# Mixing products split in stacked rows, and scans of two chunks behind a zero column with the initial state written by ScalarE into PSUM

## The chip, the cores and the metric

The kernel runs on one core of a Trainium2 chip. The metric is the device time of one launch in microseconds (us); lower is better. A core has five engines with queues of their own: TensorE (PE in the rows, its weight loads PEld), VectorE (DVE), ScalarE (ACT), GpSimd (POOL) and SyncE (SP), which here issues the DMAs. They meet through semaphores.

## The reference

A batch of 16 items (256 tokens of 512 channels, fp32) goes through a layer of self-attention, cross-attention and MLP, and then through an RWKV layer. Only the RWKV layer is touched. What matters of it, for one item (`L` = 256 tokens, 32 heads of 16 channels):

```python
xa = _ln(x)                                   # layer norm
sx = shifted(xa) - xa
t = tanh((xa + sx * maa_x) @ maa_w1).reshape(B, L, 5, 32)
m = einsum('blfd,fdc->blfc', t, maa_w2)       # five mixing products, 32 deep
xw, xk, xv, xr, xg = (xa + sx * (maa_j + m_j) for each j)
w = exp(-exp(time_decay + tanh(xw @ decay_w1) @ decay_w2))
r, k, v, g = xr @ Wr.T, xk @ Wk.T, xv @ Wv.T, silu(xg @ Wg.T)
def step(s, (k, v, w, r)):                    # scan over the 256 tokens
    a = k[..., :, None] * v[..., None, :]     # 16 x 16 per head
    out = einsum('bhs,bhst->bht', r, faaaa * a + s)
    return a + w[..., None] * s, out          # starts from s0
y = group_norm(outs);  x = x + y * g @ Wo.T;  then a gated channel mixing (fWk, fWr, fWv)
```

## The kernel before

Four phases run one after the other: self-attention (names `s_`), cross-attention (`x_`), MLP (`b_`) and RWKV (`c_`). The first three end at 2427 us and are left as they are; all that follows is in `phase_c`.

`phase_c` is a software pipeline over items, written out by hand. Call k of `body` does four parts: "wkv" is the recurrence of item k, "back" is what comes behind it for item k-1 (group norm, Wo, channel mixing, store), "front" prepares item k+1 (mixing products, projections), and "norm" prepares item k+2 (layer norm, shift, and `t`, the input of the mixing products). Calls k = -2, -1, 0 fill the pipeline, a hardware loop does k = 1 to 12 two at a time, and k = 13 to 16 are written out again; 14 and 15 lack "norm" and "front" in turn.

Each call has 16 steps, n = 0 to 15, one for each value channel of a head. A step has two halves i = 0, 1 (chunks 0-1 and 2-3 of the four chunks of 128 channels). Half (n, i) goes so: TensorE copies value channel n of each head to all 16 rows of the head, into the PSUM tile `vb` (L1649); VectorE multiplies by `kT` in place (L1478) and runs the recurrence along the 256 tokens with one scan for each chunk (L1483), which writes the states behind the initial one (`S[..., 1:T + 1]`) and reads the initial state `s0` as its operand. ScalarE puts the initial state in front, once a step (L1359). GpSimd multiplies all four chunks by `rT` (L1205), and TensorE sums over each head's rows, two steps at a time (L1660).

Between the halves, TensorE fills the four PSUM buffers `ps` in turn with everything else. Table `FILLS` (L926) sets which product stands in which step: its first list between the two halves of a step, its second behind the second half. Each fill waits until the use four before it has been emptied. ScalarE and VectorE empty the fills in the same order: what stands in the second list of step n is emptied in step n+1. The names: `g0/g1` silu gate, `mw mk mr mv mg` mixing products, `k r v` projections, `dec1 dec2` decay, `bonus`, `y` centring, `zT`, `o` Wo, `xcT`, `kk rr kv` channel mixing, `xaT` and `t`.

The mixing products (L1586) are fp32 products of `mix2` (32 to 96 rows of weights, zero where they don't belong, and a row of biases) with `tT` (tanh outputs in 96 and 64 rows and a row of ones). TensorE does an fp32 product in two instructions. The `vb` products have `float32r` operands and take one instruction; there the operand is a high part and a low part on different partitions, joined by one product. Group norm (at n = 2) is a chain through four engines: `y` to ScalarE, a sum on VectorE (L1497, L1499), a square root on ScalarE (L1367, with a table load), a reciprocal on VectorE (L1506), then five instructions of GpSimd (L1168 to L1177), and `zT` on TensorE.

SyncE's queue in a call is: load `x5`, load `s0`, load the next item's input, stack the parts of v (three DMAs), store the output. The order is fixed in `body` at L1123.

## Time and profile before

| | |
|---|---|
| median of 3 runs | 4285.62 us (4283.87 to 4286.47) |
| the profiled execution | 4279.43 us, span 4276.5 us |
| phases | attention and MLP to 2427 us; RWKV 2430 to 4276 us |
| busy over the span | PE 87%, DVE 70%, ACT 48%, POOL 41% |
| call to call of the RWKV loop | 104.3 us (L1497: 1564.1 us over 15 calls) |

The span is the stretch from the first to the last instruction of one profiled execution. A row of the timeline gives start, duration, engine, line, what is written and read, and in brackets how long the engine had been idle and what ended that. Consecutive instructions of one kind are merged (x8); an fp32 matmul counts as two. Ends of matmuls are modelled, so a duration of PE overlaps the next start: distances between starts are the safer measure.

### The profile page before, as it was taken

Reading aid. Unit: us, or ns where it says so; the run is one execution under the profiler, and the core shown is the slowest. Engines: PE = TensorE matmul, PEld = TensorE weight load, DVE = VectorE, ACT = ScalarE, POOL = GpSimd, SP = SyncE. Lnnn points to the kernel's source line nnn. Section 1 sums busy time; section 2 is a strip of 40 time slices with the busy share of each in tenths; the row PEclk is TensorE's granted clock in tenths of the full one; section 3 lists DMA queues with packets and bytes.
Section 4 is the critical chain, followed back from the end, with each engine's and each line's share of the span. In section 5 each row is a group of like instructions: output and inputs, shape, how many; then the busy total and the mean of one; then the engine's idle time right before and its main releaser. Section 6 shows DMA issues by size and latency. Waiting matters only on the chain. (4 is left out here: it accounts for less than half of the span.)

```text
span 4276.5 us, 71639 instructions
## 1 busy us (share of the span) xinstructions
PE 3728.2 (87%) x21636; PEld 2870.8 (67%) x21636; DVE 2997.0 (70%) x6732; ACT 2056.6 (48%) x5384; POOL 1740.5 (41%) x1210
## 2 busy tenths in 40 slices
PE   5998898588888886999999778999999999999976
PEld 5777777467777765899999655666666666666643
DVE  5777777477777774655655338878787877888872
ACT  4777777466767674545545422333333333333322
POOL 2444444234344341000000125666666666666652
PEclk9999999699999997999999888999999999999987
DMA  3434434244444434001001110000000000000000
GB/s 110 104 98 108 103 96 104 84 124 115 108 106 110 118 103 125 30 29 44 29 29 44 61 60 18 23 24 23 24 23 24 23 24 23 24 23 23 23 18 15
DMA packets 146611, 256.58 MB, mean 60 GB/s; under 512 B 27184, under 2 KB 32048, under 8 KB 145424
## 3 DMA queue, kind: packets, MB, share of 16 engines
q1 hardware_dynamic: 146448, 254.49, 21.9%
q8 instruction: 92, 1.51, 0.1%
q14 instruction: 71, 0.58, 0.0%
HBM read 107.62 MB, written 33.55 MB: 33 GB/s over the span
## 5 line engine op out<-in xcount | busy, mean ns | idle before, releaser
L1205 POOL TENSOR_TENSOR c_S<-c_S,c_rT 128x1024 f32<-128x1024 f32 x256 | 557.6, 2178 | 468.1 <-DVE c_S L1483 441.9
L1483 DVE TENSOR_TENSOR_SCAN c_S<-c_wT,c_s,c_vb 128x256 f32<-128x256 f32 x1024 | 708.8, 734 | 45.0 <-issue 2.7
L1478 DVE TENSOR_TENSOR c_vb<-c_kT,c_vb 128x512 f32<-128x512 f32 x512 | 352.2, 688 | 296.2 <-PE c_vb L1649 265.9
L348 POOL TENSOR_TENSOR x_prob<-x_prob,x_rsums 128x512 f32<-128x512 f32 x256 | 274.7, 1073 | 480.5 <-DVE x_rsums L510 480.5
L348 POOL TENSOR_TENSOR s_prob<-s_prob,s_rsums 128x512 f32<-128x512 f32 x256 | 274.7, 1073 | 442.0 <-DVE s_rsums L510 442.0
L1649 PE MATMUL c_vb<-c_vhl,c_spread 128*128 128x512 f32 x512 | 301.2, 598 | 73.1 <-DVE c_S L1483 60.1
L404 ACT ACTIVATE x_prob<-x_t,x_tmin 128x256 f32<-128x256 f32 x512 | 256.4, 502 | 220.5 <-DVE x_tmin L503 220.5
L404 ACT ACTIVATE s_prob<-s_t,s_tmin 128x256 f32<-128x256 f32 x512 | 256.4, 502 | 202.9 <-DVE s_tmin L503 202.9
L866 PE MATMUL b_ps<-b_ln_high,b_w_high 128*128 128x256 f32 x1024 | 290.5, 284 | 14.7 <-DVE b_ln_low L808 14.7
L867 PE MATMUL b_ps<-b_ln_low,b_w_high 128*128 128x256 f32 x1024 | 290.5, 284 | 0.0
L868 PE MATMUL b_ps<-b_ln_high,b_w_low 128*128 128x256 f32 x1024 | 290.4, 284 | 0.0
L499 DVE SCALAR_TENSOR_TENSOR s_ps_s<-s_ps_s,s_mask 128x512 f32<-128x512 f32 x256 | 177.7, 694 | 102.0 <-PE s_ps_s L596 74.9
L499 DVE SCALAR_TENSOR_TENSOR x_ps_s<-x_ps_s,x_mask 128x512 f32<-128x512 f32 x256 | 177.7, 694 | 97.0 <-PE x_ps_s L596 77.8
L1163 POOL TENSOR_TENSOR c_xmix<-c_xmix,c_xaT 128x1024 f32<-128x1024 f32 x80 | 173.9, 2174 | 144.6 <-DVE c_xmix L1427 133.2
L764 ACT ACTIVATE b_shared<-b_ps,w_cols 128x256 f32<-128x256 f32 x256 | 123.2, 481 | 207.4 <-PE b_ps L868 205.5
L503 DVE CUSTOM_DVE_ANT_0 x_t<-x_ps_s,x_mneg 128x256 f32<-128x256 f32 x512 | 197.1, 422 | 31.0 <-issue 3.3
L503 DVE CUSTOM_DVE_ANT_0 s_t<-s_ps_s,s_mneg 128x256 f32<-128x256 f32 x512 | 197.1, 422 | 29.3
L606 PE MATMUL x_ps_t<-w_ident,x_prob 128*128 128x128 f32 x1024 | 160.9, 280 | 63.2 <-ACT x_probT L414 52.2
L866 PEld LDWEIGHTS b_ps<-b_ln_high,b_w_high 128*128 128x128 f32 x1024 | 197.2, 193 | 15.7 <-ACT b_ln_high L752 15.1
L866 PE MATMUL b_ps<-b_w_high,b_act_high 128*128 128x512 f32 x512 | 201.7, 394 | 6.2 <-DVE b_act_low L829 6.1
L606 PE MATMUL s_ps_t<-w_ident,s_prob 128*128 128x128 f32 x1024 | 163.5, 284 | 45.2 <-ACT s_probT L414 36.8
L867 PE MATMUL b_ps<-b_w_low,b_act_high 128*128 128x512 f32 x512 | 199.5, 390 | 0.0
(266 smaller groups left out, 10548.7 us busy)
## 6 DMA issues: line engine op xcount, KB each, us to landing
s_stack<-s_parts_qk SPq DMA_DIRECT2D x384, 128.0 KB, 2.4
x_stack<-x_parts_qk SPq DMA_DIRECT2D x384, 128.0 KB, 2.4
s_x_in<-in_x SPq DMA_DIRECT2D x16, 512.0 KB, 3.6
s_xb<-in_x SPq DMA_DIRECT2D x16, 512.0 KB, 4.0
x<-s_x_out SPq DMA_DIRECT2D x16, 512.0 KB, 4.7
x_enc<-in_ctx SPq DMA_DIRECT2D x16, 512.0 KB, 4.4
x_x_in<-x SPq DMA_DIRECT2D x16, 512.0 KB, 3.7
x_xb<-x SPq DMA_DIRECT2D x16, 512.0 KB, 4.2
```

Of the source, the lines that this page charges most:

```text
L348: nc.gpsimd.tensor_tensor(prob[:, h % 4, :, :], prob[:, h % 4, :, :], rsums[:, h, :].unsqueeze(2).to_broadcast([P, TC, T]), ALU.mult).then ...
L404: op = nc.scalar.activation(prob[:, n % 4, tc, :], t[:, n % 2, tc, :], ACT.Exp, bias=tmin[:, n, tc:tc + 1], scale=-1.0, accum_out=psums[:, ...
L499: nc.vector.scalar_tensor_tensor(ps_s[:, n % 2, :, :], ps_s[:, n % 2, :, :], -SCALE, mask[:, :, :], ALU.mult, ALU.mult)
L503: op = nc.vector.tensor_tensor_reduce(out=t[:, n % 2, tc, :], in0=ps_s[:, n % 2, tc, :], in1=mneg[:, tc, :], scale=1.0, scalar=3.0e38, op0 ...
L606: op = nc.tensor.transpose(ps_t[:, h % 2, kc, tc * P:(tc + 1) * P], prob[:, h % 4, tc, kc * P:(kc + 1) * P], w["ident"][:, :])
L866: nc.tensor.matmul(out, sh, mh, start=start, stop=False)
L867: nc.tensor.matmul(out, sh, ml, start=False, stop=False)
L868: return nc.tensor.matmul(out, sl, mh, start=False, stop=stop)
L1205: nc.gpsimd.tensor_tensor(S[:, n % 4, :, 0:T], S[:, n % 4, :, 0:T], rT[:, par, :, :], ALU.mult).then_inc(z_ready, 1)
L1478: nc.vector.tensor_tensor(pair(vb, i), pair(kT[:, par, :, :], i), pair(vb, i), ALU.mult)
L1483: op = nc.vector.tensor_tensor_scan(S[:, n % 4, c, 1:T + 1], wT[:, par, c, :], vb[:, c, :], s0[:, par, c, n:n + 1], ALU.mult, ALU.add)
L1649: nc.tensor.matmul(pair(vb, i), spread[:, place, :], pair(vhl[:, par, slab, :, :], i), start=True, stop=True).then_inc(vb_filled, 1)
```

## The change

Three things change, all in `phase_c`.

1. The mixing products become single `float32r` products. ScalarE writes tanh into `t_low` and a rounded copy into `t_high`; VectorE leaves the difference in `t_low`; SyncE copies high, low and high parts of each of the five groups of 32 rows on top of each other into `tS` (15 DMAs of 32 rows, `stack_t`), and the weights stand in `mix2` as high, high, low, with two rows of biases. The first mixing product of the next call, `mw0`, waits for all 15 (`t_stacked`). `t` and `kv1` change places in `FILLS`.
2. The recurrence runs both chunks of a half in one scan over 512 elements. Column 0 of `wT` is zero, so the running value restarts in each chunk, and the initial state is an element of `vb`: ScalarE copies it into PSUM behind each `vb` product (`start_state`, twice a step), and VectorE's multiply waits for ScalarE (`a0_ready`) and no longer for TensorE.
3. At the start, the mixing weights are loaded three times over into a staging area (15 DMAs of 32 rows) and the biases with two DMAs of 2560 single elements; ScalarE rounds them and VectorE forms the low part before either begins with the first item. Weights wait in groups, and halving fWv moves from the end of call -2 to the end of call -1.

```diff
-             13: (["xaT0", "xaT1"], ["rr0"]), 14: (["rr1"], ["kv0"]), 15: (["kv1"], ["t"])}
+             13: (["xaT0", "xaT1"], ["rr0"]), 14: (["rr1"], ["kv0"]), 15: (["t"], ["kv1"])}
...
-        tT = sb("tT", P, 2, T)
+        MIXROWS = 3 * DM + 2
+        tS = sb("tS", MIXROWS, NMIX, T, dtype=F32R)
...
-        S = sb("S", P, 4, KC, T + 1)
+        S = sb("S", P, 4, KC, T)
...
+        t_low, t_high = b1[:, 0:2, :], b1[:, 2:4, :].bitcast(F32R)
...
-        mix2 = sb("mix2", P, NMIX, C)
+        mix2 = sb("mix2", MIXROWS, NMIX, C, dtype=F32R)
+        mix2_in = S[0:MIXROWS, :, :, :].rearrange("p b c n -> p (b c n)")[:, 0:NMIX * C]
...
 SyncE
+                for place in range(3):
+                    for block, n in ((0, 4), (1, 1)):
+                        for j in range(4 * block, 4 * block + n):
+                            sp.dma_start(staged[DM * place:DM * place + DM, j, :],
+                                         d["maa_w2"][DM * j % P:DM * j % P + DM, block, :]).then_inc(mix2_loaded, 16)
+                at = COL_AT["maa_w"]
+                for row in (3 * DM, 3 * DM + 1):
+                    sp.dma_start(mix2_in[row:row + 1, :].rearrange("o (j n) -> o j n", n=P),
+                                 d["cols"][:, at:at + NMIX * KC].rearrange("p (o j) -> o j p", o=1),
+                                 allow_slow_non_contiguous=True).then_inc(mix2_loaded, 16)
...
+                def stack_t(b):
+
+                    sp.wait_ge(tl_ready, b + 1)
+                    for j in range(NMIX):
+                        rows = slice(DM * (j % 3), DM * (j % 3) + DM)
+                        for place, x in ((0, t_high.bitcast(F32)), (1, t_low), (2, t_high.bitcast(F32))):
+                            sp.dma_start(tS[DM * place:DM * place + DM, j, :].bitcast(F32),
+                                         x[rows, j // 3, :]).then_inc(t_stacked, 16)
...
                         stack_v(k + 1, 1 - par)
+                    if "norm" in parts:
+                        stack_t(k + 2)
                     if "back" in parts:
                         sp.wait_ge(out_ready, k)
...
 GpSimd
-                            pool.wait_ge(a0_ready, step(k, n))
                             pool.wait_ge(scanned, half(k, n, 1))
-                            nc.gpsimd.tensor_tensor(S[:, n % 4, :, 0:T], S[:, n % 4, :, 0:T], rT[:, par, :, :],
+                            nc.gpsimd.tensor_tensor(S[:, n % 4, :, :], S[:, n % 4, :, :], rT[:, par, :, :],
...
 ScalarE
+                act.wait_ge(mix2_loaded, 16 * (3 * NMIX + 2))
+                nc.scalar.copy(mix2[:, :, :].rearrange("p j n -> p (j n)"), mix2_in).then_inc(mix2_high, 1)
...
-                    act.wait_ge(weights_loaded["fWv"], 16)
+
+                def half_of_last():
+                    act.wait_ge(weights_loaded[WEIGHT_GROUP["fWv"]], group_loaded("fWv"))
...
-                        nc.scalar.activation(tT[0:3 * DM, 0, :], unit(name)[0:3 * DM, 0:T], ACT.Tanh)
-                        nc.scalar.activation(tT[0:2 * DM, 1, :], unit(name)[0:2 * DM, T:2 * T], ACT.Tanh).then_inc(done, 1)
+                        for i, rows in ((0, 3 * DM), (1, 2 * DM)):
+                            op = nc.scalar.activation(t_low[0:rows, i, :], channels(name)[0:rows, i, :], ACT.Tanh)
+                        op.then_inc(done, 1)
+                        nc.scalar.drain()
+                        for i, rows in ((0, 3 * DM), (1, 2 * DM)):
+                            op = nc.scalar.copy(t_high[0:rows, i, :], t_low[0:rows, i, :])
+                        op.then_inc(th_high, 1)
...
-                def start_state(k, n, par):
-
-                    if n == 0:
+                def start_state(k, n, i, par):
+
+                    if n == 0 and i == 0:
                         act.wait_ge(s0_loaded, 16 * k + 16)
-                    if not first(k) or n >= 4:
-                        act.wait_ge(summed, k * (RS // 2) + ((n - 4) // 2 + 1))
-                    nc.scalar.copy(S[:, n % 4, :, 0], s0[:, par, :, n]).then_inc(a0_ready, 1)
+                    act.wait_ge(vb_filled, half(k, n, i))
+                    nc.scalar.copy(pair(vb, i)[:, :, 0], s0[:, par, 2 * i:2 * i + 2, n]).then_inc(a0_ready, 1)
 
                 def body(k, parts, par):
                     for n in range(RS):
+                        if "wkv" in parts:
+                            start_state(k, n, 0, par)
                         if n > 0:
                             take(k, FILLS[n - 1][1], parts, par)
...
                         if "wkv" in parts:
-                            start_state(k, n, par)
+                            start_state(k, n, 1, par)
                         take(k, FILLS[n][0], parts, par)
...
                     if isinstance(k, int) and k == -2:
                         late_weights()
+                    if isinstance(k, int) and k == -1:
+                        half_of_last()
...
 VectorE
+                dve.wait_ge(mix2_high, 1)
+                low = mix2[2 * DM:3 * DM + 1, :, :].rearrange("p j n -> p (j n)")
+                nc.vector.tensor_tensor(low, mix2_in[2 * DM:3 * DM + 1, :], low, ALU.subtract).then_inc(mix2_ready, 1)
...
-                        dve.wait_ge(s0_loaded, 16 * k + 16)
                         dve.wait_ge(w_ready, k + 1)
-                    dve.wait_ge(vb_filled, half(k, n, i))
-                    nc.vector.tensor_tensor(pair(vb, i), pair(kT[:, par, :, :], i), pair(vb, i), ALU.mult)
+                    x = pair(vb, i)[:, :, 1:T]
+                    dve.wait_ge(a0_ready, half(k, n, i))
+                    nc.vector.tensor_tensor(x, pair(kT[:, par, :, :], i)[:, :, 0:T - 1], x, ALU.mult)
                     nc.vector.drain()
...
-                    for c in (2 * i, 2 * i + 1):
-                        op = nc.vector.tensor_tensor_scan(S[:, n % 4, c, 1:T + 1], wT[:, par, c, :], vb[:, c, :],
-                                                          s0[:, par, c, n:n + 1], ALU.mult, ALU.add)
-                    op.then_inc(scanned, 1)
+                    nc.vector.tensor_tensor_scan(flat(pair(S[:, n % 4, :, :], i)), flat(pair(wT[:, par, :, :], i)),
+                                                 flat(pair(vb, i)), 0.0, ALU.mult, ALU.add).then_inc(scanned, 1)
...
                         take(k, FILLS[n][0], parts, par)
+                        if n == 15 and "norm" in parts:
+                            dve.wait_ge(th_high, k + 3)
+                            for i, rows in ((0, 3 * DM), (1, 2 * DM)):
+                                op = nc.vector.tensor_tensor(t_low[0:rows, i, :].bitcast(F32R), t_low[0:rows, i, :],
+                                                             t_high[0:rows, i, :], ALU.subtract)
+                            op.then_inc(tl_ready, 1)
...
 TensorE
                         if name == "mw0":
-                            pe.wait_ge(emptied["act"], units.emptied(k + 1, "t"))
-                            pe.wait_ge(mix2_loaded, 16 * NMIX * (KC + 1))
+                            pe.wait_ge(mix2_ready, 1)
+                            pe.wait_ge(t_stacked, 16 * 3 * NMIX * k + 2 * 16 * 3 * NMIX)
                         j = "wkvrg".index(what[1])
-                        rows = 3 * DM + 1 if j < 3 else 2 * DM + 1
                         for a in range(2):
                             c = 2 * i + a
-                            op = nc.tensor.matmul(u[:, a, :], mix2[0:rows, j, c * P:(c + 1) * P], tT[0:rows, j // 3, :],
+                            op = nc.tensor.matmul(u[:, a, :], mix2[:, j, c * P:(c + 1) * P], tS[:, j, :],
                                                   start=True, stop=True)
```

TensorE around the change of calls in the loop, before (L1576 is `t`, the second L1556 row `kv1`, L1549 with Wg `g1`, L1586 `mw0`):

```order
L1660 MATMUL c_acc<-c_S,c_gather 32x512 x4
L1556 MATMUL c_ps<-c_fWv,c_b 128x512 x4
L1647 REGISTER_ALU
L1649 MATMUL c_vb<-c_vhl,c_spread 128x512
L1576 MATMUL c_ps<-c_xmix,c_maa_w 96x256 x4
L1576 MATMUL c_ps<-c_xmix,c_maa_w 64x256 x4
...
L1649 MATMUL c_vb<-c_vhl,c_spread 128x512
...
L1549 MATMUL c_ps<-c_xmix,c_Wg 128x256 x8
L1649 MATMUL c_vb<-c_vhl,c_spread 128x512
L1580 REGISTER_ALU
L1586 MATMUL c_ps<-c_tT,c_mix 128x256 x2
```

The same place in the changed kernel, under its own line numbers (L1617 is `t`, L1597 `kv1`, L1590 `g1`, L1626 `mw0`):

```order
L1700 MATMUL c_acc<-c_S,c_gather 32x512 x4
L1617 MATMUL c_ps<-c_xmix,c_maa_w 96x256 x4
L1617 MATMUL c_ps<-c_xmix,c_maa_w 64x256 x4
L1687 REGISTER_ALU
L1689 MATMUL c_vb<-c_vhl,c_spread 128x512
L1597 MATMUL c_ps<-c_fWv,c_b 128x512 x4
...
L1689 MATMUL c_vb<-c_vhl,c_spread 128x512
...
L1590 MATMUL c_ps<-c_xmix,c_Wg 128x256 x8
L1689 MATMUL c_vb<-c_vhl,c_spread 128x512
L1622 ISA
L1626 MATMUL c_ps<-c_tS,c_mix 128x256 x2
```

Between `t` and `mw0` there were `g1` and two `vb` products; `kv1` and one more `vb` product have moved in behind `t`.

SyncE's queue from the stacking of v to the next load in the loop, in the changed kernel (before, L1137 is not there):

```order
L1121 DMA c_vhl<-c_vhl 64x1024
L1125 DMA c_vhl<-c_vlow 64x1024
L1127 ISA
L1128 DMA c_vhl<-c_vlow 64x1024
L1133 REGISTER_ALU
L1137 DMA c_tS<-c_b 32x256 x15
L1158 DMA out<-c_x 128x2x512
```

The 15 DMAs stand ahead of the store of the output and of the next call's loads.

ScalarE in steps 1 and 2 of the loop, changed kernel (L1388 is `start_state`, L1352 and L1353 empty `y`, L1398 is the square root of group norm):

```order
L1388 COPY c_vb<-c_s 128x2
L1306 REGISTER_ALU
L1352 COPY c_b<-c_ps 128x512
L1353 ACTIVATE c_b<-c_ps 128x512
L1306 REGISTER_ALU
L1352 COPY c_b<-c_ps 128x512
L1353 ACTIVATE c_b<-c_ps 128x512
L1398 ACT_TABLE_LOAD
L1398 ACTIVATE c_grstd<-c_gvar 128x64
L1387 REGISTER_ALU
L1388 COPY c_vb<-c_s 128x2
```

The initial state of half (2, 0) now stands ahead of the emptying of `y`, and that of half (2, 1) behind the square root.

## Rows read from the trace of the kernel before

**Rows 1.** Busy time by stretch: PE, PEld, DVE, ACT, POOL; granted clock, DMA share, GB/s.

```profile
3000.00:3500.00 500.00, 460.16 (x1994) 303.23 (x1994) 399.89 (x631) 158.43 (x365) 305.58 (x175) 0.98 0.08 25
```

**Rows 2.** Timeline of PE, ACT and DVE over one change of calls in the loop.

```profile
3362.03 3.70 PE L1556 MATMUL c_ps<-c_fWv,c_b 128*128 128x512 f32 x8
...
3365.80 3.76 PE L1576 MATMUL c_ps<-c_xmix,c_maa_w 128*96 128x256 f32 x16
...
3369.49 0.50 PE L1649 MATMUL c_vb<-c_vhl,c_spread 128*128 128x512 f32 x1
...
3369.60 0.38 ACT L1297 ACTIVATE c_tT<-c_ps 96x256 f32<-96x256 f32 x1 [11.67 <-PE c_ps L1576]
...
3373.51 1.89 PE L1586 MATMUL c_ps<-c_tT,c_mix 97*128 97x256 f32 x8
...
3375.05 0.59 PE L1649 MATMUL c_vb<-c_vhl,c_spread 128*128 128x512 f32 x1
...
3376.36 0.69 DVE L1478 TENSOR_TENSOR c_vb<-c_kT,c_vb 128x512 f32<-128x512 f32 x1
```

**Rows 3.** The MLP phase's timeline: float32r products of 256 columns.

```profile
1687.27 0.28 PE L867 MATMUL b_ps<-b_ln_low,b_w_high 128*128 128x256 f32 x1
1687.39 0.28 PE L868 MATMUL b_ps<-b_ln_high,b_w_low 128*128 128x256 f32 x1
```

**Rows 4.** Timeline: what PE and DVE wait for between steps 1 and 4.

```profile
3380.27 2.05 PE L1608 MATMUL c_ps<-c_centred,c_b 128*128 128x128 f32 x16 [1.48 <-DVE c_xmix L1427]
...
3387.41 0.70 DVE L1478 TENSOR_TENSOR c_vb<-c_kT,c_vb 128x512 f32<-128x512 f32 x1
3387.53 0.26 ACT L1367 ACTIVATE c_grstd<-c_gvar 128x64 f32<-128x64 f32 x1 [2.62 <-DVE c_gvar L1499]
...
3395.63 1.06 PE L1535 MATMUL c_ps<-w_ident,c_b 128*128 128x128 f32 x8 [0.48 <-POOL c_b L1177]
```

**Rows 5.** Timeline from half (5, 1) to `xcT`: its ends, and half (7, 1).

```profile
3300.24 0.69 DVE L1478 TENSOR_TENSOR c_vb<-c_kT,c_vb 128x512 f32<-128x512 f32 x1 [2.70 <-PE c_vb L1649]
...
3313.80 0.58 PE L1649 MATMUL c_vb<-c_vhl,c_spread 128*128 128x512 f32 x1
...
3314.42 0.70 DVE L1478 TENSOR_TENSOR c_vb<-c_kT,c_vb 128x512 f32<-128x512 f32 x1 [0.35 <-PE c_vb L1649]
...
3320.22 1.25 PE L1535 MATMUL c_ps<-w_ident,c_b 128*128 128x128 f32 x8 [1.58 <-DVE c_xmix L1427]
```

**Rows 6.** Timeline: the two scans of one half.

```profile
3301.01 1.38 DVE L1483 TENSOR_TENSOR_SCAN c_S<-c_wT,c_s,c_vb 128x256 f32<-128x256 f32 x2
```

**Rows 7.** ScalarE's copy of initial states: min/median/max duration in ns.

```profile
L1359 ACT COPY c_S<-c_s x256: 180/187/207, 2532.5 to 4188.9; 128x4 f32<-128x4 f32 x128
```

**Rows 8.** Timeline of SyncE's queue: twelve stacking DMAs of the attention in a row.

```profile
600.62 7.67 SPq L277 DMA_DIRECT2D s_stack<-s_parts_qk  x12
```

**Rows 9.** Loads of mixing weights: min/median/max ns of an issue; us to landing.

```profile
L1098 SPq DMA_DIRECT2D c_mix<-in_maa_w x5: 427/587/587, 2432.5 to 2444.9; - x5
...
DMA to landing us min/median/max: 2.0/2.1/3.2
```

**Rows 10.** Stretches around a wait of TensorE (columns as in rows 1).

```profile
3343.00:3345.70 2.70, 0.00 (x0) 0.00 (x0) 2.55 (x6) 1.95 (x4) 1.42 (x3) 1.00 0.00 0
3345.70:3349.00 3.30, 3.21 (x13) 1.13 (x14) 3.15 (x6) 0.68 (x2) 1.13 (x1) 0.54 0.02 5
```

**Rows 11.** Timeline of the start of the RWKV phase.

```profile
2438.24 1.29 DVE L1409 BATCH_NORM_STATS2 c_ln_stats<-c_xmix 128x6 f32<-128x512 f32 x2 [2.12 <-issue]
...
2452.20 5.23 PE L1576 MATMUL c_ps<-c_xmix,c_maa_w 128*96 128x256 f32 x16 [7.26 <-POOL c_xmix L1220]
...
2458.21 3.69 PE L1586 MATMUL c_ps<-c_tT,c_mix 97*128 97x256 f32 x16 [0.78 <-ACT c_tT L1298]
...
2471.77 1.91 ACT L1258 ACTIVATE c_fWv<-c_fWv 128x2048 f32<-128x2048 f32 x1 [7.38 <-DMA c_fWv<-in_fWv]
2473.77 1.36 PEld L1586 LDWEIGHTS c_ps<-c_tT,c_mix 65*128 65x128 f32 x4 [7.94 <-ACTq L1350]
```

**Rows 12.** A stretch of that start in which mixing weights are loaded (columns as in rows 1).

```profile
2438.60:2441.70 3.10, 0.34 (x2) 0.04 (x1) 1.42 (x6) 0.74 (x2) 0.89 (x2) 0.50 0.22 25
```

More of the change, by code:

```diff
@@ L1319, in move @@
                     elif what == "v":
[L1320 removed]
+                        nc.scalar.copy(pair(vhl[:, other, 0, :, :], i)[:, :, 1:T], channels(name)[:, :, 0:T - 1]).then_inc(vh_ready, 1)
                     elif what == "y":
@@ L1684 @@
              "fWr": (KC, C), "fWv": (KC, C)}
+WEIGHT_GROUP = {n: i for i, names in enumerate((("maa_w1",), ("decay_w1", "decay_w2", "Wk", "Wr", "Wv"),
+                                                ("Wg", "Wo", "fWk", "fWr", "fWv"))) for n in names}
 def build_program(nc, d, out):
```

53 lines of the change are left out of this document (24 added, 29 removed).

## The prediction

> **What bounds the kernel now.** I first read the page (its busy shares stand in the table above), then the busy time by stretch, then the timeline of one call, since the change touches only the RWKV phase. In its loop TensorE is busy 460 of 500 us, VectorE 400, GpSimd 306, ScalarE 158 [rows 1]. That looks like a kernel bound by TensorE, and a change that takes instructions off TensorE looks like pure gain. The timeline says more. The reader should look at who waits in which steps of a call (104.3 us). TensorE waits for VectorE at `y` in step 1 [rows 4], for GpSimd's end of group norm at `zT` in step 4 [rows 4], and for VectorE again at `xcT` in step 8 [rows 5]. Between these places VectorE runs almost without a gap: from half (1, 0), which starts at 3376.36 [rows 2], to half (2, 1) at 3387.41 [rows 4], and from half (5, 1) at 3300.24 to `xcT` at 3320.22, with one wait of 0.35 us at half (7, 1) [rows 5]. So a call is a relay: VectorE and group norm set the pace from the change of calls to `zT`, TensorE from `zT` to half (5, 1), VectorE from there to `xcT`, mostly TensorE after that. The change of calls itself runs without a wait: `t`, then `vb`, `g1`, `vb`, and `mw0` [rows 2].
>
> **What is removed from TensorE, and where it stands.** A call has five mixing products of four matmuls, each in two instructions. Eight of these instructions (`mw0`, `mw1`) take from 3373.51 to 3375.05, 1.54 us [rows 2]; over the x8 row's own 1.89 us at most. After the change four float32r products remain, 0.12 us apart [rows 3], 0.48 us. That is 1.1 us (up to 1.4) for each of five products, 5.5 to 7 us a call. On the path is little of it. `mw` counts, 1.1 us, because half (1, 0) stands behind it. `mk`, `mr` and `mg` lie where TensorE waits for VectorE or for `zT` afterwards [rows 4, 5], and `mv` stands at the head of the VectorE stretch, where its time ends in the 0.35 us wait of half (7, 1).
>
> **What is added at the change of calls.** I count from the end of `t`, the moment at which ScalarE could read it. Before, TensorE spent 3369.49 to 3373.51 on `vb`, `g1`, `vb`, 4.0 us [rows 2]; `kv1` and another `vb` now come in behind `t`, 3362.03 to 3365.80, 3.8 us [rows 2]. That is 7.8 us of cover for the new chain, which goes so:
> - the `vb` product of half (15, 1) and its initial state on ScalarE: 0.6 us from a `vb` to VectorE's start [rows 5], and one copy, 0.19 us [rows 7]: 0.8.
> - VectorE multiplies and scans half (15, 1), 0.7 and 1.3 us [rows 5, 6]; ScalarE's two tanh (0.38 each [rows 2]) and two copies of the same size lie beside it: 2.0.
> - VectorE's two subtractions, of 256 elements; a multiply of 512 takes 0.69 [rows 5], so half of that and a little: 0.4 each, 0.8. SyncE wakes in about 0.1 (my estimate). 3.7 so far.
> - 15 DMAs, issued by one queue. An issue of 32 rows takes 0.43 to 0.59 us [rows 9], and twelve stacking DMAs of the attention, SBUF to SBUF over 32 rows as these are, take 7.67 us, 0.64 each [rows 8]. I take 0.55, between the two: the attention's carry four times the bytes. Fourteen intervals are 7.7 us; the ends are 6.0 and 9.0.
> - the last one lands 2.1 us after its issue [rows 9].
> The sum is 3.7 + 7.7 + 2.1 = 13.5 us against 7.8 of cover: `mw0` waits about 5.7 us (ends 4.0 and 7.0). Behind `mw0` in TensorE's queue stand `mw1`, half (1, 0), the row sums that `y` needs, and all of step 1; VectorE has finished half (0, 1) and `g1` by then and waits too.
>
> TensorE's clock adds to it. After a wait of 2.7 us the granted clock is 0.54 over the next 3.3 us [rows 10], so the half level, 1.2 of 2.4 GHz, for most of them. `mw` and a `vb` then take some 0.4 us more.
>
> So half (1, 0) starts on TensorE at +5.7 - 1.1 + 0.4 = +5.0. On VectorE it was 1.3 us behind TensorE [rows 2] because VectorE was late; it will be 0.9 behind, with ScalarE's hand-over in it: +4.6.
>
> The Trainium skill gives the price of an issue otherwise: "DMA: Bandwidth & Descriptors", Anatomy of one DMA, has about 50 ns of sequencer dispatch, small descriptor generation and a fixed cost of about 2 us, for DMAs issued by GpSimd. The 2 us agree with the trace (2.1), the 50 ns do not (427 to 587 ns on SyncE). By the page's figure the 15 issues would take under 1 us and the chain would be covered; that is rival B below, whose price comes from rows.
>
> **The scans and the initial state.** Two scans of a half take 1.38 us [rows 6]; one over 512 elements saves one instruction's fixed part. Bounds: nothing, and 0.3 us. I take 0.1, since the second scan of the pair starts with the first not yet ended. VectorE had 32 of them a call, 3.2 us, but on the path are the four between half (1, 0) and (2, 1), -0.4, and six up to `xcT`, -0.6. The new hand-over, `vb` to ScalarE to VectorE, is 0.2 to 0.4 us wherever VectorE waits for TensorE: half (5, 1) is on the path, +0.3; the wait of 0.35 at (7, 1) goes, -0.3. Half (11, 1) leads to the late half (13, 0): +0.3 - 0.2. In step 2 ScalarE's state for half (2, 1) stands behind the square root, which ended at 3387.79, while VectorE began that half at 3387.41 [rows 4]; with a copy and a hand-over, +0.7. In steps 3 and 4 the emptying of `dec2` and `zT` moves behind a state each: +0.3. GpSimd loses a wait that did not bind. Sum of this paragraph: +0.1 us.
>
> **Per call:** 4.6 + 0.1 = 4.7 us; 14 calls of the loop and behind it (k = 1 to 14) have `mw0`: +66 us. At k = 0 there is no `kv1` and no half (15, 1): the chain from `t` is 0.7 + 0.7 + 0.8 + 0.1 + 7.7 + 2.1 = 12.1 against 4.0 of cover, 8.1, less 1.1 and with 0.4 as above: +7.
>
> **The start.** VectorE's first statistics began at 2438.24, `t` at 2452.20, `mw0` at 2458.21, and the fifth to eighth of the mixing products waited until 2473.77, because ScalarE stood behind the load of fWv [rows 11]. That wait goes. New: 15 loads of 32 rows at 0.48 to 0.59 us from 2432.5 on end at about 2440.5. Two DMAs of 2560 single elements follow. In 3.1 us before, five DMAs with 512 single elements and 64 KB kept the DMA engines busy 22% [rows 12], 10.9 engine-us; ten times that over 16 engines is 6.8 us, more if fewer engines share it: landed at about 2450. ScalarE's rounding of 2560 columns (2048 took 1.91 [rows 11]): 2.4; VectorE's subtraction of 2560: 2.8. So statistics at 2455, 17 us late, `t` at 2469, `mw0` 18 us behind it instead of 6 (5.3 for `t`, then 12.1) at 2487, and what restarted at 2473.77 comes 8 us behind that: +21 us. Ends: +8 if the elements land with the rest, +45 if they go through few engines.
>
> **Sum:** 66 + 7 + 21 = +94 on the profiled execution's 4279.4 us, 4373; the median of the runs lies 6 us higher, at 4285.6: **4380 us**, slower by 2.2%. The last two calls gain or lose under 5.
>
> **Rivals.**
> A. *TensorE's time counts.* If the busy share tells the truth, a call shortens by the 5.5 to 7 us taken off TensorE and the queue hides its DMAs: 14 x -6 = -84, +15 at the start, 4217 us. For it: 92% busy. Against it: the three waits above, and that the DMAs must all land before the first product.
> B. *The DMAs are covered.* Issues come at 0.1 us, as if no engine's queue held them up; the chain is 3.7 + 1.4 + 2.1 = 7.2 under 7.8 of cover. Then `mw` finds VectorE busy as before, a call changes by about +0.1, and the start is +13: 4300 us.
> C. *The queue is as slow as in the attention and the clock stays low.* 0.64 us an issue, `mw0` waits 7.0, and group norm's square root and row sums run late at 1.2 GHz (1.2 us more): 7.0 - 1.1 + 0.4 - 0.4 + 0.1 + 1.2 = +7.2 a call, 101, with 10 at k = 0 and 35 at the start: 4432 us. It decides from 0.6 us an issue on.
> D. *The start is dearer.* The two element DMAs run through few engines, 45 us: 4404 with the rest as forecast.
>
> **Chances.** Forecast 0.55, A 0.08, B 0.08, C 0.17, D 0.12. The forecast's own range is 4345 to 4415 (issues 0.43 to 0.64, start +10 to +30). The range for 8 in 10 reaches down towards B and up to C: 4310 to 4440. Under 0.2% (9 us) cannot be told from no change; faster by more than that: A, and a little of B, 0.09; within: 0.04; slower: 0.87.
>
> **What would show it.** Right: an idle time of TensorE ahead of `mw0` in each call, 4 to 7 us, ended by a DMA of `tS`; SyncE's 15 issues in a row over 7 to 9 us; a call of 109 us for 104.3; TensorE's busy share down to about 83% in the loop; mixing products 0.12 us apart; a scan of 1.2 to 1.35 us. At the start, `t` near 2469 and the first mixing product near 2487. Wrong: `mw0` without a wait, or a wait there and the time given back between `zT` and `xcT`, which I say is set by VectorE and GpSimd.

## The result and the profile after

The changed kernel takes 4469.4 us (median of 4 runs, 4464.4 to 4478.5) where the kernel before takes 4284.7 in the same job: 1.0439 times as long, 95% interval 1.0418 to 1.0460. Slower was right; the size was not. I had forecast 4380 and a range up to 4440: +94 us, and it is +185.

The profiled execution has a span of 4467.5 us against 4276.5. Its RWKV phase begins 6.8 us later than before, by the earlier phases alone (first load at 2436.99, was 2430.16), so the phase itself lost 184.2. The busy times by stretch of the changed kernel (columns as in [rows 1]):

```profile
3000.00:3500.00 500.00, 427.18 (x1733) 276.39 (x1732) 355.39 (x446) 156.77 (x411) 290.94 (x158) 0.90 0.09 25
```

TensorE went from 460 to 427 us busy in 500, with 1733 instructions for 1994; its granted clock went from 0.98 to 0.90 of full speed. Every engine is busy for less of the time: none of them became the bound, they all wait more.

The change of calls, to be laid beside [rows 2]: TensorE's, VectorE's, GpSimd's and SyncE's rows of the timeline (start, duration, engine, line, what it writes from what; in brackets the idle time before it and who ended it).

```profile
3374.37 3.84 PE L1617 MATMUL c_ps<-c_xmix,c_maa_w 128*96 128x256 f32 x16
...
3378.48 3.59 PE L1597 MATMUL c_ps<-c_fWv,c_b 128*128 128x512 f32 x8
...
3382.14 3.62 PE L1590 MATMUL c_ps<-c_xmix,c_Wg 128*128 128x256 f32 x16
3385.41 0.58 PE L1689 MATMUL c_vb<-c_vhl,c_spread 128*128 128x512 f32 x1
3394.49 1.22 PE L1626 MATMUL c_ps<-c_tS,c_mix 98*128 98x256 f32 x4 [8.51 <-DMA c_tS<-c_b]
```

```profile
3379.64 1.22 DVE L1519 TENSOR_TENSOR_SCAN c_S<-c_wT,c_vb 128x512 f32<-128x512 f32 x1
3380.78 2.90 DVE L1546 TENSOR_TENSOR c_b<-c_b 96x256 fp32r<-96x256 f32 x2
...
3380.94 2.46 POOL L1226 TENSOR_TENSOR c_S<-c_S,c_rT 128x1024 f32<-128x1024 f32 x1 [6.50 <-DVE c_S L1519]
...
3383.70 9.45 SPq L1137 DMA_DIRECT2D c_tS<-c_b  x15
```

The reader should see the chain of the forecast, link by link: `t`, the half (15, 1) on VectorE, the two subtractions, 15 DMA issues in a row, and TensorE with nothing to do for 8.51 us. Two links are longer than I had them. The subtractions take 2.90 us, not 0.8, and they stand beside a multiply on GpSimd. The issues take 9.45, 0.63 each, not 0.55.

The start of the phase (beside [rows 11]), ScalarE, VectorE, TensorE and the DMA queue:

```profile
2446.32 3.29 SPq L1111 DMA_DIRECT2D c_S<-in_cols  x2
2449.64 17.02 SPq L1100 DMA_DIRECT2D c_decay_w<-in_decay_w  x2
...
2474.71 2.32 ACT L1265 CAST c_mix<-c_S 98x2560 fp32r<-98x2560 f32 x1 [30.07 <-DMA c_S<-in_cols]
...
2477.06 2.82 DVE L1439 TENSOR_TENSOR c_mix<-c_S,c_mix 33x2560 fp32r<-33x2560 f32 x1 [33.97 <-ACT c_mix L1265]
2481.98 1.29 DVE L1445 BATCH_NORM_STATS2 c_ln_stats<-c_xmix 128x6 f32<-128x512 f32 x2 [2.10 <-issue]
...
2514.32 2.05 PE L1626 MATMUL c_ps<-c_tS,c_mix 98*128 98x256 f32 x8 [13.18 <-DMA c_tS<-c_b]
```

and the DMA engines in stretches of it (the last two figures are the DMA engines' busy share and GB/s):

```profile
2450.00:2455.00 5.00, 0.00 (x0) 0.00 (x0) 0.00 (x0) 0.00 (x0) 0.00 (x0) 0.50 1.24 1
2455.00:2460.00 5.00, 0.00 (x0) 0.00 (x0) 0.00 (x0) 0.00 (x0) 0.00 (x0) 0.50 1.24 1
2460.00:2465.00 5.00, 0.00 (x0) 0.00 (x0) 0.00 (x0) 0.00 (x0) 0.00 (x0) 0.50 1.33 0
```

The second of the two DMAs of 2560 single elements is issued at 2447.4, and ScalarE, which waits for both, starts at 2474.71, 27 us later. In between the DMA engines move 1 GB/s or less in the stretches shown, with a mean busy share above 1 over the 16 of them (the times of packets overlap, so the share alone does not tell how many engines work). The next load, of decay_w, stays 17 us at the head of the queue, and the norm statistics, which need none of this, stand on VectorE behind the subtraction that waits for it.

To find where a call lost its time I took the starts of TensorE's groups in eleven calls of the loop and the median of each gap (worked out from the timelines; us; the last column is the whole call). `kv1` moved into the first gap and out of the last, 3.8 us.

```
                t-mw0  -y   -dec1  -k0   -zT   -o0   -r0  -bonus -xcT  -v0  ..  -t    call
before           7.7   6.8   3.3   5.3   6.8   5.9   5.7   14.2   4.1  2.4      8.5  105.5
the change      20.1   5.6   3.8   4.0   8.4   7.6   4.5   12.9   5.7  2.6      4.8  115.6
mixing alone    19.9   5.6   3.3   4.0   8.0   5.9   4.5   12.9   6.1  4.2      4.8  114.7
scans alone      7.7   6.6   3.2   5.3   7.6   6.2   5.7   14.2   3.9  2.4      8.5  106.6
all repaired    11.5   6.6   3.8   4.3   8.0   6.0   4.5   12.9   5.7  3.8      4.8  108.3
scans, state
 by VectorE      7.7   6.6   3.2   5.3   6.8   5.9   5.7   14.2   3.8  2.4      8.5  104.5
```

A call gets 8.6 us longer in the first gap (12.4 less the 3.8 of `kv1`). Four other gaps, which hold the five mixing products, get 1.1 to 1.3 us shorter (`mw` and `mk` share the one before `y`). Against that the gaps before `zT`, `o0` and `xcT` get 1.6 to 1.7 us longer each. Before `zT` and `xcT` these are waits for GpSimd and VectorE; before `o0` it is TensorE's clock, as the rows at `zT` will show below.

### The profile page after: what moved, and what is told of

Same layout as the page of the kernel before. It is cut to its first block and busy times, and to the rows that moved or that the text cites. A ratio compares the mean times of both kernels' runs of the same rounds, so it can differ in the third digit from the quotient of the medians.

```text
span 4467.5 us, 71098 instructions
## 1 busy us (share of the span) xinstructions
PE 3720.9 (83%) x21316; PEld 2848.0 (64%) x21316; DVE 2964.6 (66%) x6253; ACT 2101.5 (47%) x5673; POOL 1787.6 (40%) x1212
## 5 line engine op out<-in xcount | busy, mean ns | idle before, releaser
L1226 POOL TENSOR_TENSOR c_S<-c_S,c_rT 128x1024 f32<-128x1024 f32 x256 | 605.1, 2364 | 456.5 <-DVE c_S L1519 456.5
L1388 ACT COPY c_vb<-c_s 128x2 f32<-128x2 f32 x512 | 83.7, 163 | 1232.5 <-PE c_vb L1689 1232.0
L1519 DVE TENSOR_TENSOR_SCAN c_S<-c_wT,c_vb 128x512 f32<-128x512 f32 x512 | 625.0, 1221 | 50.8 <-issue 8.3
L1515 DVE TENSOR_TENSOR c_vb<-c_kT,c_vb 128x510 f32<-128x510 f32 x512 | 351.7, 687 | 455.1 <-ACT c_vb L1388 422.5
L1689 PE MATMUL c_vb<-c_vhl,c_spread 128*128 128x512 f32 x512 | 302.1, 599 | 71.8 <-DVE c_S L1519 56.9
```

The lines of the kernel that those rows point to most:

```text
L1226: nc.gpsimd.tensor_tensor(S[:, n % 4, :, :], S[:, n % 4, :, :], rT[:, par, :, :], ALU.mult).then_inc(z_ready, 1)
L1515: nc.vector.tensor_tensor(x, pair(kT[:, par, :, :], i)[:, :, 0:T - 1], x, ALU.mult)
L1519: nc.vector.tensor_tensor_scan(flat(pair(S[:, n % 4, :, :], i)), flat(pair(wT[:, par, :, :], i)), flat(pair(vb, i)), 0.0, ALU.mult, ALU.ad ...
L1689: nc.tensor.matmul(pair(vb, i), spread[:, place, :], pair(vhl[:, par, slab, :, :], i), start=True, stop=True).then_inc(vb_filled, 1)
```

## The experiments

| kernel | median us | times before (95%) |
|---|---|---|
| the change | 4469.4 | 1.0439 (1.0418 to 1.0460) |
| e1 mixing alone | 4452.8 | 1.0399 (1.0382 to 1.0417) |
| e2 scans alone | 4301.6 | 1.0045 (1.0025 to 1.0064) |
| e3 change, own wait for w | 4405.1 | 1.0281 (1.0258 to 1.0303) |
| e4 change, subtractions early | 4441.9 | 1.0362 (1.0341 to 1.0384) |
| e5 scans alone, rT padded | 4291.6 | 1.0023 (1.0010 to 1.0036) |
| e6 change, rows by transpose | 4443.6 | 1.0384 (1.0366 to 1.0403) |
| e7 change, early and three waits | 4347.8 | 1.0152 (1.0133 to 1.0171) |
| e8 mixing alone, repaired | 4313.3 | 1.0082 (1.0063 to 1.0102) |
| e9 change, all repaired | 4316.9 | 1.0094 (1.0079 to 1.0110) |
| e10 scans, padded, state by VectorE | 4253.8 | 0.9943 (0.9929 to 0.9956) |
| e11 e9 with o1 early | 4317.7 | 1.0094 (1.0078 to 1.0109) |
| e12 before with o1 early | 4280.4 | 1.0007 (0.9997 to 1.0017) |
| e13 change, state by VectorE | 4424.4 | 1.0341 (1.0317 to 1.0364) |
| e14 e9, state by VectorE | 4275.9 | 0.9997 (0.9986 to 1.0009) |
| e15 change, filler of 32 | 4546.4 | 1.0620 (1.0596 to 1.0644) |
| e16 change, filler of 16 | 4454.5 | 1.0428 (1.0408 to 1.0448) |
| e17 scans, state by VectorE | 4268.5 | 0.9977 (0.9967 to 0.9988) |

A hundredth in the ratio is 43 us. Differences between kernels of different jobs are taken from the ratios.

**The two halves alone (e1, e2).** e1 is the change with the lines of `start_state`, `recur`, `S` and the zero columns as before; e2 is the kernel before with those lines of the change.

> The change without its scans: the stacked mixing, the grouped weight semaphores and the exchange of t and kv1 are in, the state still goes into column 0 of S and the scans are two of 256 as before. My theory (the loss lies in the wait for the 15 DMAs that stack t, 8.7 us a call, and in the start): the whole loss stays and the small gain of the merged scans goes, about 4480 us, 1.045 of the kernel before, and the wait of TensorE for tS stays near 8.7 us. Rival (the hand-over of the column through ScalarE, which now stands between TensorE and VectorE in each of 32 halves, costs some 3 us a call): 4420 us or less, and the period of a call falls from 116 to 113 us.

> The kernel before with the scans of two chunks, the zero column and the state written by ScalarE into PSUM, and nothing else; mixing as before. My theory: 0.4 to 0.9 us a call are gained where half-steps wait for each other, 4270 to 4280 us, 0.997 to 0.999 of the kernel before. Rival (the hand-over through ScalarE costs): 4310 to 4335 us, with the period of a call 2 to 3 us longer than 105.8 us.

The stacked mixing costs 171 us by its ratio. The scans, of which I had expected a gain, cost 19 (1.0045), and 17 on top of the mixing (1.0439 less 1.0399). The losses add up. Both of my expectations on the scans were wrong; e2 fell between my range and the rival's.

**The wait for the stacked t (e3, e4, e7).**

```diff
 e3: x[rows, j // 3, :]).then_inc(t_stacked if j else w_stacked, 16)
     mw0 waits for w_stacked, mk0 for t_stacked
 e4: the block "if n == 15 ... tl_ready" moved ahead of recur(k, n, 1, par)
 e7: e4, and three semaphores: j = 0, j = 1, j = 2 to 4;
     ScalarE's copy of y0 waits for the third, since it overwrites t
```

> The change with two semaphores for the stacking DMAs: the first mixing product waits for its own three DMAs alone, and the second group's (k) for the other twelve. My theory: 12 issues of 0.63 us leave the wait of mw0 (8.7 us a call becomes about 1.2) and TensorE keeps its clock; at least 15 x 7.5 = 113 us are gained, up to 150 with the clock: 4320 to 4356 us. What is left over before is then the start (about 50 us) and 1 to 2 us a call. Rival (the landing of a DMA or the late subtraction makes the wait, not the queue of issues): the wait stays above 5 us and the time above 4410 us.

> The change with the two subtractions that make t_low put ahead of VectorE's multiply and scan of half (15,1), so that they no longer stand beside GpSimd's multiply of S and rT. Theory (an operation of VectorE that reads both inputs from SBUF waits while GpSimd works on SBUF): both subtractions together fall from 2.9 to under 1.2 us, t is low 2 to 3 us earlier, and 15 calls gain 30 to 45 us: 4425 to 4440 us. Rival (2.4 us is what the 64x256 subtraction to float32r costs in any place): no gain, 4465 us or more.

> The change with the subtractions ahead of the last half's multiply and with three semaphores for the stacked t: the w product waits for its 3 DMAs, the k product for its 3, the rest for the other 9 (ScalarE's copy of y, which overwrites t, too). Theory (queue of 15 issues and nothing else): from t to the first w product 20.1 us become 11.5 to 12.3, the 9 us from there to y (with one semaphore for the other twelve) become 5.6, the period of a call falls from 116 to 107 to 108, the clock goes back to 0.97, 4469 - 15 x 8 to 9 = 4335 to 4350 us. Rival (VectorE's and GpSimd's chains through the same stretch would be the next wait): period 110 or more, above 4375 us.

e3 gave 68 us by the ratios (1.0439 less 1.0281), not 113: the time from `t` to `mw0` fell by 7.5 us as expected, and 3.4 of them came back between `mw0` and `y` (5.6 to 9.0), because `mk0` waits for the same queue (2.2 us in the call shown, 5.6 in every second one):

```profile
3363.03 0.74 PE L1628 MATMUL c_ps<-c_tS,c_mix 98*128 98x256 f32 x4 [1.34 <-DMA c_tS<-c_b]
...
3370.36 1.22 PE L1628 MATMUL c_ps<-c_tS,c_mix 98*128 98x256 f32 x4 [2.15 <-DMA c_tS<-c_b]
```

In e4 the two subtractions take 0.75 us, and GpSimd's multiply comes after them:

```profile
3372.92 0.75 DVE L1540 TENSOR_TENSOR c_b<-c_b 96x256 fp32r<-96x256 f32 x2 [4.00 <-ACT c_b L1327]
...
3375.65 2.35 POOL L1226 TENSOR_TENSOR c_S<-c_S,c_rT 128x1024 f32<-128x1024 f32 x1 [8.52 <-DVE c_S L1519]
```

That gave 33 us, as expected: the same instructions took 2.1 us less for standing elsewhere. e7, both together, gave 123 us. With it `mw0` and `mk0` have no wait for a DMA left from the second call of the loop on; the first gap is 11.45 us, that is the 7.73 of before and the 3.8 of `kv1`. So the 8.6 us of the first gap were the queue of 15 issues and the late subtraction, and nothing else. One part of what I expected did not come: the granted clock went back to 0.93 only (3000 to 3500), not to 0.97.

**The start (e6).**

```diff
-   sp.dma_start(<row>, d["cols"][...].rearrange("p (o j) -> o j p", o=1))   # 2560 elements, twice
+   TensorE: transpose of the 20 columns; ScalarE: copy to SBUF
+   sp.dma_start(<row>, b2[0:NMIX * KC, 0, 0:P])                             # 20 pieces of 512 bytes, twice
```

> The change, with its two rows of offsets made otherwise: TensorE transposes the 20 columns once, ScalarE copies them out, and each row is loaded by one DMA of 20 pieces of 512 bytes in place of 2560 elements. Theory (the start is long because 2 x 2560 elements are slow and hold the DMA queue, and VectorE's norm statistics stand behind the mixing weights' subtraction): the load is in about 25 us earlier, the statistics start near 2456 instead of 2482, and 25 to 40 us are gained: 4430 to 4445 us. Rival (the start is set by the later weights or by the norm): under 10 us gained.

24 us by the ratios, just under the 25 to 40 that I had expected. From the first load to the first group norm sum the trace has 248.9 us for 272.5. The load of decay_w leaves the queue at once:

```profile
2438.99 1.72 SPq L1111 DMA_DIRECT2D c_S<-c_b  x2
2440.76 1.09 SPq L1100 DMA_DIRECT2D c_decay_w<-in_decay_w  x2
```

**The scans' loss (e5, e10, e17, e13).**

```diff
 e5:  rT = sb("rT", P, 2, KC, T + 1), used in [0:T]
 e10: e5, and in recur, after the wait for vb_filled:
+     nc.vector.tensor_copy(pair(vb, i)[:, :, 0], s0[:, par, 2 * i:2 * i + 2, n])
      start_state and its two calls on ScalarE left out
 e17: e10 without the padding of rT.   e13: the change with e10's copy.
```

> The kernel with the scans alone (4301.6 us, 16.6 above before), with one unused column behind each row of 256 in rT, so that GpSimd's multiply of S and rT has again one operand in separate rows. In the traces GpSimd's 128x1024 multiply takes 2.18 us where S has rows of 257 and 2.36 us where all operands lie close; 16 a call make 2.9 us of GpSimd. Theory 1 (the 17 us come from GpSimd): the multiply takes 2.18 us again and the time falls to 4283 to 4290 us. Theory 2 (they come from the hand-over of the column through ScalarE, ahead of other work of its queue): the multiply may fall, the time stays at 4297 to 4303 us.

> The kernel with the scans alone and rT in padded rows (4291.6 us), but the initial state is copied into the zero column of PSUM by VectorE itself, ahead of its multiply, and ScalarE has no part in it. Theory (what is left over the kernel before, 10 us, is the hand-over TensorE to ScalarE to VectorE in 32 halves a call and what waits behind it in ScalarE's queue): 4270 to 4284 us, at most the kernel before. Rival (the hand-over is free, the copy on VectorE costs its own 0.1 us 512 times): 4292 us or more.

> The change with one edit: VectorE copies the initial state into the zero column itself, ScalarE has no part in it. With the scans alone this edit brought 38 us (4291.6 to 4253.8). Theory (the price of the hand-over is per half-step and holds here too): 4425 to 4440 us. Rival (here the waits for the stacked t set the pace and cover the hand-over): 4455 us or more.

> The scans alone with the state copied by VectorE, rT without its padding, so GpSimd's multiply of S and rT takes 2.36 us again. If the padding is worth what it was beside ScalarE's hand-over (10 us), 4260 to 4268 us against 4253.8 with it. Rival (the padding counted only because ScalarE's queue was late): 4250 to 4257 us.

GpSimd's multiply of S and rT, in the kernel with the scans alone, with the padding, and with VectorE's copy but without padding (grouped instructions: line, operands, count, then busy us and mean ns):

```profile
L1207 POOL TENSOR_TENSOR c_S<-c_S,c_rT 128x1024 f32<-128x1024 f32 x256 | 604.0, 2359 | 438.8 <-DVE c_S L1486 438.8
```

```profile
L1207 POOL TENSOR_TENSOR c_S<-c_S,c_rT 128x1024 f32<-128x1024 f32 x256 | 557.4, 2177 | 456.2 <-DVE c_S L1486 456.0
```

```profile
L1207 POOL TENSOR_TENSOR c_S<-c_S,c_rT 128x1024 f32<-128x1024 f32 x256 | 604.2, 2360 | 442.8 <-DVE c_S L1477 442.6
```

One unused column in rT makes the same multiply 8% faster. It is worth 0.34% without ScalarE's hand-over (e17 against e10). Beside the hand-over it is 0.22% (e5 against e2), between my two theories for e5 and with intervals that overlap, so not shown there by itself. The hand-over is the larger part: taking ScalarE out brings 0.80% (e10 against e5), 0.68% without the padding (e17 against e2), and 0.98% inside the change (e13). One way in which it acts shows at `zT`. First the changed kernel, then e13:

```profile
3416.34 1.36 PE L1576 MATMUL c_ps<-w_ident,c_b 128*128 128x128 f32 x8 [1.79 <-POOL c_b L1199]
...
3417.36 0.78 PE L1689 MATMUL c_vb<-c_vhl,c_spread 128*128 128x512 f32 x1
...
3417.93 4.83 PE L1590 MATMUL c_ps<-c_xmix,c_Wk 128*128 128x256 f32 x16
3418.17 0.16 ACT L1388 COPY c_vb<-c_s 128x2 f32<-128x2 f32 x1 [0.74 <-PE c_vb L1689]
3418.27 1.93 ACT L1296 ACTIVATE c_b<-c_ps,w_cols 128x256 f32<-128x256 f32 x4
...
3420.28 2.35 POOL L1207 TENSOR_TENSOR c_b<-c_b,c_g2T 128x1024 f32<-128x1024 f32 x1 [1.75 <-ACT c_b L1296]
```

```profile
3386.51 1.06 PE L1567 MATMUL c_ps<-w_ident,c_b 128*128 128x128 f32 x8 [1.78 <-POOL c_b L1199]
3387.17 1.93 ACT L1296 ACTIVATE c_b<-c_ps,w_cols 128x256 f32<-128x256 f32 x4 [0.86 <-PE c_ps L1567]
...
3387.64 3.62 PE L1581 MATMUL c_ps<-c_xmix,c_Wk 128*128 128x256 f32 x16
...
3389.18 2.36 POOL L1207 TENSOR_TENSOR c_b<-c_b,c_g2T 128x1024 f32<-128x1024 f32 x1 [0.49 <-ACT c_b L1296]
```

ScalarE's copy of two columns takes 0.16 us and counts for little. But it waits for the `vb` product that stands behind `zT` in TensorE's queue, and the emptying of `zT`, long ready, stands behind the copy: 1.93 us after `zT` begins instead of 0.66, and GpSimd's product with the gate comes 3.94 us after it instead of 2.67. Over the whole execution VectorE waits for the copies longer than it waits in e13 for TensorE itself. In us, times, longest, first the change, then e13:

```profile
DVE c_vb L1515 <- ACT c_vb L1388: 422.5, 201, 7.7
```

```profile
DVE c_vb L1505 <- PE c_vb L1680: 351.8, 167, 7.7
```

The Wo product comes 7.57 us after `zT` in the changed kernel and 5.90 in this call of e13, but that difference is not the hand-over. It is TensorE's clock. The k product between the two takes 4.83 us instead of 3.62, and the granted clock (the figure before the last two) is 0.66 against 1.00, first the change, then e13:

```profile
3417.00:3422.00 5.00, 5.00 (x19) 4.24 (x18) 2.30 (x3) 2.45 (x6) 3.25 (x2) 0.66 0.00 0
```

```profile
3387.00:3392.00 5.00, 5.00 (x32) 3.80 (x30) 3.14 (x6) 2.52 (x5) 4.51 (x3) 1.00 0.00 0
```

e7, which keeps the hand-over, has both: 5.95 us in nine of 14 calls, 7.58 in five. The changed kernel has 7.57 in all 14, e13 in five. So part of the 42 us that e13 gained came with the clock (nine calls of 1.65 us are 15 us), and how the rest divides over the steps is not shown. What the runs show is the price of the hand-over as a whole.

Without it the merged scans are what I had thought them, a gain: e10 is 0.57% faster than before (I had expected at most 0.35%), the best kernel of the study.

**What the saved TensorE time is worth (e8, e9, e14, e11, e12).** e8 is e1 with the repairs of e7 and e6; e9 is the change with these and the padding; e14 is e9 with the state copied by VectorE; e11 and e12 are e9 and the kernel before with step 5 as `(["o0"], ["o1"])`, step 6 as `(["r0"], ["mv0", "mv1"])` and GpSimd's addition for v in step 6.

> The stacked mixing alone (scans and state as before; 4452.8 us as it was) with all three repairs: rows by transpose, subtractions early, three semaphores. Theory: 30 us less at the start and 8 to 9 us less in each of 15 calls: 4290 to 4305 us, equal to or a little above before (4285 us), since the TensorE time that the stacking saves (5 us a call) is no bound. Rival (TensorE's saved time counts once the waits are gone): 4240 us or less. Rival 2 (new waits): 4340 us or more.

> The whole change with all four repairs: rows by transpose, subtractions early, three semaphores for the stacked t, rT in padded rows. If the costs add up as the runs so far have them (4469.4 of the change, less 121.7 for the semaphores and the early subtractions, less 25.8 for the rows, less 10 for the padding): 4312 us, still 1.006 to 1.008 of the kernel before. Rival (with the waits gone the 5 us a call of saved TensorE time and the merged scans show at last): 4270 us or less.

> The whole change with its four repairs (4316.9 us) and the state copied by VectorE. Theory (38 us again): 4275 to 4290 us, so slower than the scans alone in the same form (4253.8 us): the stacked mixing costs some 25 us even when repaired, by the start and by norm and gate chains that do not shorten. Rival (on the faster scans TensorE becomes the bound and its saved 5 us a call count): 4240 us or less.

> The change with all four repairs, and the product o1 moved ahead of the mixing products of v (and GpSimd's addition for v one step later). Theory (TensorE's saved time between o0 and xcT is given back as the wait for the second norm, a chain that begins with o1: bonus to xcT 5.65 us against 4.05 before): the chain starts 3 us earlier, the wait at xcT goes, and 2 to 3.5 us a call return, 28 to 50 us less than the same kernel without the move: 4265 to 4285 us if that is 4312. Rival (another chain sets xcT or the next projection): under 10 us gained.

> The kernel before with the same move of o1 alone. Theory: TensorE waits there only 1.6 us a call for xcT, so at most 14 x 1.6 = 22 us: 4262 to 4278 us. If the move brings as much here as in the repaired change, the saved TensorE time was not what made room for it.

The costs add up (e9: 4312 expected, 4316.9 measured; e14: 4275 to 4290, 4275.9); e8, at 4313.3, came 8 us above its range. And the rival that had TensorE's time count fell three times: with all repairs the stacking still costs 0.54% on top of e10 (0.9997 against 0.9943), although each of the five mixing products of a call is about 1.1 us shorter. Of the 8 us between the RWKV phases of their two profiled executions, 6 lie before the first group norm sum. My own theory of where that time goes fell with e11. Moving `o1` did nothing, in either kernel: the gap from `bonus` to `xcT` went from 5.7 to 5.3 us only. The rows name another cause. `xcT` waits for VectorE's reading of the g mixing product (it takes over that product's place in PSUM), with a wait of 1.58 us before [rows 5] and of 1.76 us in the changed kernel,

```profile
3330.61 0.66 PE L1576 MATMUL c_ps<-w_ident,c_b 128*128 128x128 f32 x4 [1.76 <-DVE c_xmix L1463]
```

in both cases with halves of the scan ahead of that reading on VectorE. No run took that wait away, so it is named, not shown.

**The clock (e15, e16).**

```diff
+ for _ in range(32):      # e16: 16
+     nc.tensor.matmul(u[:, 0, :], w["ident"][:, :], same_u[:, 0:2, :], start=True, stop=True)
  pe.wait_ge(mix2_ready, 1)      # mw0, which then overwrites u
```

> The change with 32 idle products of 128x256 (about 7 us at the full clock) ahead of the first mixing product's wait, written to the place that it then overwrites; nothing else differs. Theory (part of the 10 us a call is the half clock after the wait: y 3.6 us instead of 2.1, k1 4.8 instead of 3.6, and the places zT and o0 that come 1.6 us later each): the granted clock of the stretch 3000 to 3500 rises from 0.90 to 0.96 or more, and 2 to 3 us a call come back: 4425 to 4440 us. Rival (TensorE's clock falls where others set the pace): the clock rises and the time stays above 4460 us.

> As the filler before, with 16 idle products in place of 32: 16 x 0.425 = 6.8 us, which end inside the wait of 8.7 us. Theory (from the filler of 32: y to dec1 and the product w to y became 0.6 us shorter each once the clock was up, the place zT to o0 did not): 1.2 us a call, 18 us: 4445 to 4458 us. Rival 1 (no part of the loss is the clock): 4463 us or more. Rival 2 (the products delay what waits in front of them, such as the first half's broadcast): above 4480 us.

e15 asked nothing: its 32 products took 13.6 us where I had reckoned 7, and so were themselves the wait. e16 is the test. The filler ends inside the wait and the clock in the loop is 0.96 for 0.90:

```profile
3029.70 7.07 PE L1622 MATMUL c_ps<-c_same_u,w_ident 128*128 128x256 f32 x32
...
3038.34 0.74 PE L1629 MATMUL c_ps<-c_tS,c_mix 98*128 98x256 f32 x4 [1.57 <-DMA c_tS<-c_b]
```

```profile
3000.00:3500.00 500.00, 446.27 (x1907) 296.87 (x1907) 360.73 (x448) 155.16 (x408) 293.27 (x158) 0.96 0.10 27
```

The medians differ by 15 us, which is inside the range that I had expected, but the four runs spread from 4441 to 4471 and the intervals of the ratios overlap (1.0428 and 1.0439). By the medians alone the low clock costs between nothing and 2 us a call. The calls of the profiled execution, the fastest of the four, say more. In five of 14 calls the clock is low behind `zT`, as it is in all 14 of the change. Without the first call of the loop, these take 115.2 to 115.6 us and the others 112.6 to 113.6. So where the clock stays up a call of this kernel is some 2 us shorter. In e7, whose calls are shorter, the same comparison shows no clear gain (108.8 against 105.2 to 109.7).

## Why the prediction was right in kind and half in size

Three terms of the sum were too small: the wait of `mw0` (5.7 us, measured 8.7 on average), the scans with ScalarE's hand-over (+0.1 us a call, measured about +1.1), and the start with k = 0 (+28 us, measured +57). The clock behind `zT` and GpSimd's longer multiply had no term. The steps, as the prediction put them:

- **A call is a relay; TensorE's busy time is no bound.** Right, and the firmest result: rival A, which took the time off the call, is refuted by e8, e9 and e14.
- **The saving on the path is 1.1 us, at `mw`.** Right in size: `mw0` to `y` is 1.1 us shorter, although `mk` stands in this gap too. Of the others, `k0`, `r0` and `bonus` come 1.2 us earlier each after `dec1`, `o0` and `r0`, and 3.2 are given back before `zT` and `xcT` (1.6 at each).
- **`mw0` waits 5.7 us.** Mis-sized: 8.5 in nearly every call, 8.7 on average over k = 1 to 14. The chain was right, two terms were not: 15 issues at 0.63 us rather than 0.55 (+1.1), which is the attention's 0.64 of [rows 8] and not the middle between it and [rows 9]; and 2.9 us for the subtractions that I had put at 0.8 (+2.1), by the size of the operation and without looking at what ran on GpSimd beside them. Small terms, such as a landing of 1.9 us for 2.1, give 0.4 back. I had rival C decide from 0.6 us an issue on; it did, though its 4432 us fell short too.
- **The clock, +0.4.** Mis-sized. Behind `mw0`, where I had put it, e16 has 0.7 us less up to `y`. Behind `zT` I had none, and there it is 1.65 us in every call of the change. Rival C had 1.2 for a clock that stays low.
- **Scans and state, +0.1 a call.** Wrong: about +1.1 a call (e2). The scan's saving was underrated: with both losses removed e10 gains 24 us, 1.5 a call, where I had 1.0 on the path. The hand-over I had as 0.2 to 0.4 us at a few halves, with +0.3 for what stands behind it in steps 3 and 4; it costs 29 to 42 us, about 2 a call, part of it with the clock. And I had no term at all for GpSimd's multiply, whose operand lost its row gaps: 0.18 us in 16 multiplies a call, worth about 15 us (e17 against e10).
- **The start, +21, and k = 0, +7.** Mis-sized. Less the offset of 6.8, the products that restarted at 2473.77 [rows 11] restart at 2522.34: +41.8. Up to the first group-norm sum (2645.8, now 2709.5) it is +56.9, so k = 0 has the other 15. I had scaled the element DMAs from 3.1 us in which other loads ran too [rows 12], to 6.8 us; they took more than 20. Rival D had the start dear too, by few engines; which engines worked the trace does not tell. It shows 5120 elements, slow on a mean share above 1, and a queue that stands still behind them.

The sum nearly closes: 29 us more at the start and k = 0, 3.0 us more of wait in 14 calls (42), and 17 for the scans less the 1.4 that I had for them make 87, and 94 forecast plus 87 is 181 against 185 measured. That it comes so close is partly luck, since it leaves out both the clock behind `zT` (14 times 1.65, 23 us) and what the shorter mixing products kept. That the sign and half of the size came out right was no luck: the chain at the change of calls was read link by link. Three prices were too low at once, all for operations that [rows 1] to [rows 12] do not show in the company in which they now run.

## What to carry to other kernels

Put a small copy that waits on one engine's newest product into the queue of the engine that needs the result, not into a third engine's queue, where everything behind it inherits the wait: here that edit turned a loss of 0.45% into a gain of 0.23% (e2 to e17), and with the padding into one of 0.57% (e10). A batch of small DMAs costs its issues in a row, so give the first consumer a semaphore of its own and make nobody wait for the last one who needs the first. And price an instruction with the neighbours that it will have, not with those of the row from which its duration is read.
